# Three orders of work in the first attention of a fused transformer kernel, and later row statistics in the second

## What is computed

```python
x = x + attn_a(layernorm(x))   # 16 heads of 16; q.k over 2048 rows, softmax, then
                               # opt = sum over m of att[l, m] * v[l]; opt @ w_out.T + b_out
x = x + ffn(layernorm(x))      # y = relu(x @ W_fc.T)**2 @ W_proj.T; five steps of a
                               # spiking neuron with constant input y; mean of the spikes
x = x + attn_b(layernorm(x))   # 16 heads over a reinterpreted layout, a temperature per head
x = x + ffn(layernorm(x))
```

## Time and profile before

| | us |
|---|---|
| Median of 3 runs | 2729.12 (2728.18 to 2730.86) |
| The profiled execution | 2727.77 |
| Its span, first to last instruction | 2726.0 |
| Mean granted TensorE clock, share of full speed | 0.979 |

### The profile page before, as it was taken

How to read it: one execution, slowest core, us unless ns; L and a number is a source line. 1 busy time by engine, 2 the same in 40 slices (tenths; PEclk the granted TensorE clock), 3 DMA queues, 4 the chain that set the end, 5 groups by cost and what they waited for, 6 DMA issues and landing times. The chain is left out here.

```text
span 2726.0 us, 39855 instructions
## 1 busy us (share of the span) xinstructions
PE 2310.4 (85%) x12453; PEld 1084.6 (40%) x12672; DVE 2501.0 (92%) x3626; ACT 2558.9 (94%) x4763; POOL 1279.9 (47%) x1891
## 2 busy tenths in 40 slices
PE   5788888877777777777778899999999999999998
PEld 2244444433433433443342334343433434333434
DVE  5899999999999999999988999999999999999995
ACT  4899999999999999999998999999999999999994
POOL 0146566654554554554552244444344444434444
PEclk8799999999999999999999999999999999999999
DMA  7511212133211111111111111111011111111110
GB/s 212 124 55 50 82 52 72 49 93 87 64 35 43 33 35 40 38 35 35 51 33 41 49 43 35 41 45 46 29 47 44 36 39 45 43 31 47 44 30 16
DMA packets 190938, 140.84 MB, mean 52 GB/s; under 512 B 92163, under 2 KB 177669, under 8 KB 190726
## 3 DMA queue, kind: packets, MB, share of 16 engines
q1 hardware_dynamic: 190406, 137.69, 18.4%
q10 hardware_dynamic: 320, 0.59, 0.1%
HBM read 92.04 MB, written 41.94 MB: 49 GB/s over the span
## 5 line engine op out<-in xcount | busy, mean ns | idle before, releaser
L1059 DVE TENSOR_REDUCE nmax<-score 128x1 f32<-128x1024 f32 x1024 | 1196.7, 1212 | 105.7 <-PE score L823 98.8
L1032 DVE TENSOR_SCALAR_CACHE_REDUCE big<-score 128x1024 f32<-128x1024 f32 x1024 | 1194.7, 1217 | 48.2 <-PE score L761 45.5
L1264 ACT ACTIVATE big<-big,nmax 128x1024 f32<-128x1024 f32 x1024 | 1168.1, 1143 | 36.8 <-DVE big L1032 33.1
L1306 ACT ACTIVATE score<-score,nmax 128x1024 f32<-128x1024 f32 x1024 | 1119.8, 1100 | 45.7 <-DVE nmax L1059 44.5
L823 PE MATMUL score<-big,shared 128*128 128x512 bf16 x1956 | 619.7, 397 | 271.3 <-ACT score L1306 236.4
L761 PE MATMUL score<-shared 128*128 128x512 bf16 x1921 | 534.6, 382 | 57.5 <-DVE big L1032 40.3
L742 PE MATMUL bank_g<-big,qw 128*32 128x512 f32 x4096 | 492.6, 599 | 1.0 <-ACT qcol L1291 1.0
L823 PEld LDWEIGHTS score<-big,shared 128*128 128x128 bf16 x2048 | 130.2, 98 | 566.1 <-ACT score L1306 474.0
L761 PEld LDWEIGHTS score<-shared 128*128 128x128 bf16 x2048 | 165.3, 98 | 429.1 <-DVE big L1032 253.9
L717 PE MATMUL bank_f<-norms,w_fc_sb 128*128 128x128 f32 x2048 | 297.1, 278 | 45.5 <-ACT hid L1228 44.5
L717 PEld LDWEIGHTS bank_f<-norms,w_fc_sb 128*128 128x128 f32 x2048 | 278.5, 192 | 114.0 <-ACT hid L1228 75.3
(11 more groups left out here) (147 smaller groups left out, 1747.5 us busy)
## 6 DMA issues: line engine op xcount, KB each, us to landing
shared<-q_parts SPq DMA_DIRECT2D x256, 64.0 KB, 2.4
shared<-kb_parts SPq DMA_DIRECT2D x256, 64.0 KB, 2.2
shared<-vb_parts SPq DMA_DIRECT2D x256, 64.0 KB, 2.2
big<-k_parts SPq DMA_DIRECT2D x48, 192.0 KB, 5.1
big<-k_parts SPq DMA_DIRECT2D x24, 256.0 KB, 7.9
kb_parts<-pieces SPq DMA_DIRECT2D x96, 64.0 KB, 1.6
vb_parts<-pieces SPq DMA_DIRECT2D x96, 64.0 KB, 1.6
shared<-in_x SPq DMA_DIRECT2D x32, 128.0 KB, 2.3
```

The source lines that it names most:

```text
L1032: v.tensor_scalar(row_chunk(c), score_b(turn, c)[:, :], -1.0, INF, ALU.mult, ALU.min, accum_out=nmax[:, par, c // NCH, c % NCH:c % NCH + 1 ...
L1059: v.tensor_reduce(nmax[:, par, c // NCH, c % NCH:c % NCH + 1], score_a(turn, c)[:, :], AX.X, ALU.max, negate=True).then_inc(max_a, 1)
L1264: a.activation(row_chunk(c), row_chunk(c), ACT.Exp, bias=nmax[:, par, c // NCH, c % NCH:c % NCH + 1], scale=-1.0, accum_out=esum[:, par, c ...
L1306: a.activation(s[:, :], s[:, :], ACT.Exp, bias=nmax[:, par, c // NCH, c % NCH:c % NCH + 1], accum_out=esum[:, par, c // NCH, c % NCH:c % N ...
```

## The change

The chunks at which steps are issued in the first attention become entries of three plans. `BESIDE` is the order of before. `LATE` serves iterations 3 to 10, `ALONE` iterations 11 to 30; 0 to 2, 31, 32 and the rest that runs into the second attention keep `BESIDE`. TensorE, VectorE and ScalarE take their chunks from the plan; the order within POOL's and SP's programs stays as it is. In iterations 3 to 9 the slice statistics, means and normalisations are split over chunks, in iteration 2 they stay; in 3 to 10 the first value product moves to chunk 3, the first key product to 4, and the take of the slice's queries to 9. In the second attention L977 and L982 move from chunks 24 and 25 to 27 and 28. No instruction is added or removed.

```diff
-KV_A, Q_A = [13, 14, 15, 16], [18, 20]
-
-UP_A, UP_B = [18, 19, 20, 21, 22, 23, 24, 25], [1, 1, 2, 2, 4, 4, 5, 5]
-
-DOWN_A, DOWN_B = [26, 26, 27, 27, 28, 29, 30, 30], [17, 17, 18, 18, 19, 19, 20, 20]
+BESIDE = dict(turn_opt=9, out=[10, 11], turn_x2=12, kv=[13, 14, 15, 16], q=[18, 20],
+              turn_x1=17, up=[18, 19, 20, 21, 22, 23, 24, 25], down=[26, 26, 27, 27, 28, 29, 30, 30],
+              fac=1, take_opt=7, take_x2=10, take_x1=15, take_k=15, take_v=15,
+              take_q=[20, 20], relu=[19, 23], take_y=29,
+              rec=4, add=11, stats_x1=12, mean_x1=13, stats_x2=6, mean_x2=7)
+LATE = dict(turn_opt=7, out=[10, 10], turn_x2=12, kv=[13, 13, 14, 15], q=[20, 22],
+            turn_x1=17, up=[18, 19, 19, 21, 23, 23, 23, 24], down=[26, 27, 27, 28, 29, 29, 30, 30],
+            fac=0, take_opt=7, take_x2=10, take_x1=15, take_k=14, take_v=16,
+            take_q=[22, 24], relu=[20, 23], take_y=29,
+            rec=4, add=10, stats_x1=11, mean_x1=12, stats_x2=0, mean_x2=6)
+SLICE_EARLY = dict(stats=[14, 14], mean=16, norm=[25, 25])
+SLICE_LATE = dict(stats=[12, 16], mean=18, norm=[23, 24])
+SLICE_V, SLICE_KQ, TAKE_SLICE_Q = [3, 5], [4, 6, 8, 9], 9
+ALONE = dict(turn_opt=7, out=[8, 9], turn_x2=10, kv=[12, 13, 15, 15], q=[17, 19],
+             turn_x1=18, up=[19, 21, 21, 21, 23, 23, 24, 24], down=[26, 26, 27, 28, 29, 30, 31, 31],
+             fac=0, take_opt=5, take_x2=9, take_x1=17, take_k=14, take_v=14,
+             take_q=[19, 30], relu=[20, 23], take_y=30,
+             rec=3, add=9, stats_x1=14, mean_x1=15, stats_x2=1, mean_x2=5)
...
+        def plan(it):
+
+            if NE - 1 <= it < N_STEPS:
+                return LATE
+            return ALONE if N_STEPS <= it < T - 1 else BESIDE
...
-                if c in (4, 5):
-                    s = c - 4
+                if c in SLICE_V:
+                    s = SLICE_V.index(c)
...
-                if c in (3, 6, 8, 9):
-                    m = (3, 6, 8, 9).index(c)
+                if c in SLICE_KQ:
+                    m = SLICE_KQ.index(c)
...
-                        if c == 9:
+                        if c == at["turn_opt"]:
...
-                        if c == 24:
+                        if c == 27:
                             ffn_stats_of(T + i1, (quad + 3) % 4, x3_ready, i1 + 1)
-                        if c == 25:
+                        if c == 28:
                             ffn_mean(T + i1)
...
-                if c == 8:
+                if c == TAKE_SLICE_Q:
                     act.wait_ge(s_q, u + 1)
...
                     a.activation(kvf[:, 0:D], bank_q[:, 0:D], ACT.Copy, scale=temp_sb[:, bass.ds(i3, 1)])
+                if c == at["take_v"]:
                     a.activation(kvf[:, D:2 * D], bank_q[:, D:2 * D], ACT.Copy).then_inc(qkv_kvf, 1)
```

More of the change, by code:

```diff
@@ L807, in phase_a @@
                 w, u, g = step_at(it), slice_at(it), group_at(it)
+                at = plan(it)
                 if i is not None:
@@ L949, in slice_aggr, with slice_norm @@
                     v.bn_aggr(s_mv[:, s, :], s_stat[:, s, :]).then_inc(s_aggr, 1)
-            def slice_norm(u):
-                dve.wait_ge(s_rstd, 2 * u + 2)
-                need(dve, s_tr, u)
-                dve.wait_ge(s_aggr, SLS * u + SLS)
-                for s in range(SLS):
-                    last = v.tensor_scalar(s_n[:, s, :], s_x[:, u % 2, s, :], s_mv[:, s, 0:1], s_rs[:, s:s + 1],
-                                           ALU.subtract, ALU.mult)
-                last.then_inc(s_xn, 1)
+            def slice_norm(u, s):
+                if s == 0:
+                    dve.wait_ge(s_rstd, 2 * u + 2)
+                    need(dve, s_tr, u)
+                    dve.wait_ge(s_aggr, SLS * u + SLS)
+                last = v.tensor_scalar(s_n[:, s, :], s_x[:, u % 2, s, :], s_mv[:, s, 0:1], s_rs[:, s:s + 1],
+                                       ALU.subtract, ALU.mult)
+                if s == SLS - 1:
+                    last.then_inc(s_xn, 1)
             stats(0)
@@ L1067, in phase_a @@
                             v.tensor_tensor(nrow[:, :], nmax[:, r1, :, 0], nmax[:, r1, :, 1], ALU.min).then_inc(att_min, 1)
[L1068 removed]
+                        if c == at["rec"]:
                             dve.wait_ge(att_sum, 2 * i1 + 2)
                             v.reciprocal(rec[:, :], tot[:, :]).then_inc(att_rec, 1)
[L1071 removed]
+                        if c == at["add"]:
                             dve.wait_ge(oproj, i1 + 1)
@@ L1078, in phase_a @@
                             v.tensor_tensor(xin[:, r1, :], bank_f[:, D:2 * D], xa[:, r1, :], ALU.add).then_inc(ffn_x1, 1)
-                        if c == 12:
+                        if c == at["stats_x1"]:
                             ffn_stats_of(i1, r1, ffn_x1, i1 + 1)
-                        if c == 13:
+                        if c == at["mean_x1"]:
                             ffn_mean(i1)
                     if i3 is not None:
-                        out_stats(i3, r3, c)
+                        out_stats(i3, r3, c, at)
                     ahead = next_slice(it)
                     if ahead is not None:
-                        if c == 14:
-                            slice_stats(ahead)
-                        if c == 16:
+                        at_s = SLICE_LATE if u is not None else SLICE_EARLY
+                        for s in range(SLS):
+                            if c == at_s["stats"][s]:
+                                slice_stats(ahead, s)
+                        if c == at_s["mean"]:
                             slice_aggr(ahead)
-                        if c == 25:
-                            slice_norm(ahead)
+                        for s in range(SLS):
+                            if c == at_s["norm"][s]:
+                                slice_norm(ahead, s)
             iterations(phase_a)
@@ L1285, in project_b @@
                     a.activation(kvf[:, 0:D], bank_q[:, 0:D], ACT.Copy, scale=temp_sb[:, bass.ds(i3, 1)])
+                if c == at["take_v"]:
                     a.activation(kvf[:, D:2 * D], bank_q[:, D:2 * D], ACT.Copy).then_inc(qkv_kvf, 1)
-                if c == 20:
-                    act.wait_ge(qkv_q, i3 + 1)
-                    need(act, qb_stored[r], 8 * (i3 - r))
-                    for m in range(KC):
+                for m in range(KC):
+                    if c == at["take_q"][m]:
+                        if m == 0:
+                            act.wait_ge(qkv_q, i3 + 1)
+                            need(act, qb_stored[r], 8 * (i3 - r))
                         last = a.activation(attention_q(i3, r)[:, m * P:(m + 1) * P], bank_q[:, m * P:(m + 1) * P],
                                             ACT.Identity, bias=bqb_col[:, m:m + 1])
-                    last.then_inc(qkv_qf, 1)
+                        if m == KC - 1:
+                            last.then_inc(qkv_qf, 1)
             def phase_a(it, turn, _):
```

77 lines of the change are left out of this document (38 added, 39 removed).

## The result

The changed kernel takes **2663.67 us** (median of 4 runs, 2661.41 to 2666.28) against 2728.65 (4 runs, 2728.18 to 2730.86) for the kernel before: a ratio of 0.9761, with a 95% interval of 0.9744 to 0.9778. That is 65 us less where 49 were forecast; the sum was 2680, and the range's lower end, 2664, lies just above the measured time. The direction and the three places were right, and the gain was forecast too small in two of them, by 5.2 of 21.5 us and by 8.1 of 25.1. The profiled execution took 2661.41 (span 2659.6).

A forecast was written before the change was run, and what follows sets the result against it. ScalarE was taken to bound the kernel (busy 94%), or VectorE (92%) where ScalarE waits for it. Gains 16.3 + 17.0 + 15.8 = 49.1 us off 2727.77 gave 2678.7, plus 1.35 for the median: 2680; range 2664 to 2706.

The forecast's parts named there:

- the 0.68, 0.58 and 0.72: Slice iterations: ScalarE's idle us before the turned output's copy (chunk 7) and before exponentials behind the slice statistics and normalisations.
- I leave 0.15 of the 0.58: Slice iterations: with the statistics split to chunks 12 and 16, 0.15 us of ScalarE's 0.58 wait remains, 0.43 returned.
- I leave 0.2 of the 0.72: Slice iterations: with the normalisations at chunks 23 and 24, 0.2 us of ScalarE's 0.72 wait remains, 0.52 returned.
- I leave 0.05 of the 0.27: Slice iterations: the relu waits one chunk longer, so 0.05 us of ScalarE's 0.27 wait before the first relu remains.
- the hidden part: ScalarE's waits for VectorE hardly shown as idle, 0.04 to 0.05 us a chunk; about 0.35 returned per slice iteration.
- So of 0.77 I leave 0.22: Iterations 11 to 30: of ScalarE's 0.77 us idle per iteration 0.22 remains and 0.55 returns, besides 0.3 hidden.
- The remark on SP's queue: Iterations 11 to 30: SP stands until the query take at chunk 30, six stores before its next loads; priced at nothing.
- (a): Slice iterations: both normalisations block beside POOL, 2.27 us instead of 1.61, 4.6 less gain, 2685; chance 0.12.
- (b): Iterations 11 to 30: half clock in all twenty, 10.9 us dearer, 2691, chance 0.10; in none, 2675, chance 0.08.
- (c): First attention: late rows and packed ups lose what VectorE gives; only 15.8 us gained, 2713; chance 0.07.
- (d): Second attention: POOL's late normalisation outruns VectorE's last minimum; 2.4 us x 31 = 74 lost, 2770; chance 0.02.
- (e): Whole change: a plan that is not used would be no change; chance 0.01.

The follow-up runs named there:

- the late statistic alone: Kernel before with only the second attention's statistics and mean moved to chunks 27 and 28: 2708.74 us, ratio 0.9936.
- the kernel before with products: Kernel before with seven added products, one behind each score of chunks 2 to 8 of iterations 11 to 30, result unused: 2729.51 us, ratio 0.9997.
- the two combined versions: Changed kernel plus six products, new plan for iteration 31, spread slice steps in iteration 2: 2662.92 us; with iteration 31's takes at chunk 20: 2652.59 us.

## Why the prediction was right in its direction and short in its size

**Slice iterations: 21.5, forecast 16.3.** The mechanism was right: the 0.68, 0.58 and 0.72 are gone. What failed is the size of two terms: the remainders ("I leave 0.15 of the 0.58", "I leave 0.2 of the 0.72", "I leave 0.05 of the 0.27") and the hidden part, "about 8 x 0.045 = 0.35". The windows show both. Idle time fell from 2.30 to 0.00 an iteration, where 1.85 was taken; ScalarE's busy time fell by 291.63 / 7 - 287.60 / 7 = 0.58, where 0.35 of hidden time was taken. Together 2.88 against 2.2. The starts of the exponentials in iteration 5 show where the waits had been priced too low. An idle time in brackets is less than what the wait costs. Before, exponentials 7 and 8 start 2.19 us apart, 14 and 15 1.78, 25 and 26 1.93. Less the pace of 1.09, and at chunk 7 the copy of 0.27, that is 0.83, 0.69 and 0.84, where the brackets have 0.68, 0.58 and 0.72: the rest is hidden in recorded durations. After, the same three distances are 1.35, 1.46 (with the copy of the keys in it) and 1.09. The normalisations of 0.40 fit into the lead and cost nothing. The statistics still cost something, the 0.23 before exponential 13, but without a bracket; the 0.15 that the prediction left for them was no bad guess, and the low prices of the other waits outweighed it. What else helped was the copy of the keys at chunk 14, which fills the wait behind the statistics, as the run with VectorE's order old shows; the prediction gave it no price. Its bound of 22 for the stage held, though its 0.65 of hidden time per iteration was not worked out from any row; 0.58 was measured.

**Iterations 11 to 30: 25.1, forecast 17.0.** Two sizes were off. The steady iteration went from 40.05 to 38.92, so 1.13 x 20 = 22.6; 0.85 was taken. "So of 0.77 I leave 0.22" is the step: 0.07 was left (38.92 - 38.85), and busy time fell by 0.39 instead of 0.3. The other part is the clock. The prediction counted six iterations at 0.78, 4.7 us; the kernel before had nine of 40.58 to 40.85 and one of 40.32, together 807.56 - 20 x 40.05 = 6.6. After the change it is 782.42 - 20 x 38.92 = 4.0, so 2.5 us came from there. The forecast had put nothing on that.

**Second attention: 16.2, forecast 15.8.** The mechanism was right; that the number came so close is partly luck. VectorE's wait for POOL's sum is gone in all iterations, the steady one takes 39.13 (0.27 less), the late kind has disappeared, and POOL's cover was 1.24 us. How much a late statistic returns depends on how many late iterations the kernel before has, and that varies: iterations 33 to 62 took 1199.8, 1202.7, 1206.2 and 1209.1 in the four profiles with the statistic at 24. And the kernel after lost 2.5 us in iteration 33 against the late statistic alone.

**What was costed at nothing.** Iterations 0 to 2, 31 and 32, which have the old plan, became 3.3 us shorter in the profile. In 0 to 2 most of it is one stretch at half clock at the start of iteration 2 (44.80 before, 43.11 after). The late statistic alone, which has the old plan throughout the first attention, shows 43.10 there; the kernel before with products shows 44.82, and the two combined versions, built on the changed kernel, have the stretch again. It comes and goes, and no run makes it an effect of the change. The remark on SP's queue, "Price nothing", was right for the iterations that have the plan and would have been wrong by 6.9 us for the next one.

**The rivals.** (a) *Both normalisations block*: neither did, 0.41 and 0.40. But the mechanism is real, and one chunk earlier both were held and took back 0.63 an iteration. The Trainium skill, SBUF — State Buffer, section Who interferes with whom, has VectorE in its two-port modes and GpSimd hold a shared pair of ports exclusively, with the second to issue blocked fully. That a normalisation is held until just after POOL's TENSOR_TENSOR ends agrees; the one at 307.50, inside a POOL TENSOR_SCALAR and not held, does not. The one at 307.44 with the normalisations at 22 and 23 is recorded 0.03 us before POOL's count and was held all the same. No run shows in which mode VectorE ran. The prediction had also read a minimum of 0.555 from the earlier trace rows as the unblocked time: the shortest of fourteen need not be an undisturbed one. It is 0.40 alone. (b) *The clock*: the number of affected iterations stayed near the same, and each lost less, at most 0.64 instead of 0.8. The cost of all of them is measured at 3.8 us. (c) *The first attention only moves its waits*: it gave 46.6 of the 66.4. (d) *Slower by POOL's late normalisation*: not at 27, but at 30 it happened: the second attention became 66 us longer than before, where 74 was its price; part of the 66 was half clock, which the price did not have. (e) fell with the first window.

## What to carry to other kernels

Where two engines pass rows to each other at nearly the same pace, a small step of one costs little if it falls where the other has a copy of its own to run, and nearly its whole length where the lead is used up (0.69 us for 0.74 of statistics). So take the cost of a wait from the starts of the instructions around it and not from its idle time alone, and look for a copy that can be moved into it. In the slice iterations all idle time plus the busy time above the free pace (22 us) came closer to the 21.5 measured than the idle times less a remainder for each (16.3). Move the consumer and its producer together (the early add without the early product made the kernel slower than before), and follow each moved step into the in-order queues, above all at the iteration that ends a phase. A wait for another engine that is only just met is worth three chunks of distance even where its mean cost is small, since it is what makes executions differ; but measure the cover on the far side, which here was 1.2 us.

## What the runs showed of the hardware

- **Recorded durations of ScalarE can hide a wait.** In iteration 5 after the change exponentials with nothing between them start 1.09 us apart (282.16 to 283.25, 312.30 to 313.39), while their recorded durations go from 1.09 to 1.22. At 295.73, 1.32 us after the one before, the duration is back at 1.09 and no idle time is recorded. Only the starts tell the pace, and only they show that wait.
- **A VectorE normalisation of 0.40 us took 0.9 to 1.1 beside some POOL instructions and 0.41 beside another**: beside the square and the count (TENSOR_TENSOR) it ended 0.15 us after POOL did, wholly inside the spike step (TENSOR_SCALAR) it was not held. The second of a pair at chunk 25 takes 0.555; in all 54 such cases a spike step begins 0.01 to 0.02 us after it (321.38 against 321.36 in the kernel before). Why that costs 0.15 was not settled.
- **The granted clock fell after a few chunks of nothing but scores**: in iteration 17 TensorE was busy for 1.64 of the 3.41 us before the fall to 1.2 GHz. Six products of 128x256 with no reader kept it at 2.4 GHz in all of iterations 12 to 30. In the kernel before, seven such products left three of twenty iterations with a fall. These three falls come 0.2 to 0.4 us into the iteration, before the first added product (chunk 2). Why the other seventeen have none stays open.
- **With the statistic at chunk 24 the second attention has no fixed length**: the late iterations appeared in other numbers and lengths in each of four profiles (35 to 62 took 1112.2, 1115.0, 1118.2 and 1119.6), a spread of 7 us that hid the gain of the products, and with it at 27 the same stretch took 1095.8 or 1095.9 in nine.
